# Two scalar loads moved to ScalarE's DMA queue, and the first rows loaded in four pieces

## What is computed

```python
x = x + jnp.tanh(g_xattn[0]) * _L0_xattn_ref(_layernorm(x), ctx_2048)
x = x + jnp.tanh(g_ffn[0]) * _L0_ffn_ref(_layernorm(x), Wg, w1, w2)
# _L0_xattn_ref: both operands rounded to fp8 by blocks, then a product
xq = quant_dequant_act_1x128(x)             # one scale for each row and 128 columns
wq = quant_dequant_weight_128x128(weight)   # one scale for each 128 by 128 block
return jnp.einsum('emk,enk->emn', xq, wq)
# _L0_ffn_ref: softmax router, top 2 of 8 experts, capacity 640 rows for each expert
h = jax.nn.relu(jnp.einsum('ecd,edf->ecf', dispatched, w1))
expert_out = jnp.einsum('ecf,efd->ecd', h, w2)
```

## Time and profile before

| | us |
|---|---|
| median of 3 runs (lowest, highest) | 882.12 (880.8, 883.58) |
| span of the profiled execution, first to last instruction | 888.7 |
| PE busy in the span | 812.6 (91%) |
| DVE busy | 606.8 (68%) |
| ACT busy | 365.3 (41%) |
| POOL busy | 236.2 (27%) |
| chain that ended last: PE, DVE, ACT, issue, DMA | 80%, 10%, 3%, 3%, 2% |

### The profile page before, as it was taken

How to read it: one execution, slowest core, us unless ns; L and a number is a source line. 1 busy time by engine, 2 the same in 40 slices (tenths; PEclk the granted TensorE clock), 3 DMA queues, 4 the chain that set the end, 5 groups by cost and what they waited for, 6 DMA issues and landing times.

```text
span 888.7 us, 12025 instructions
## 1 busy us (share of the span) xinstructions
PE 812.6 (91%) x4249; PEld 387.7 (44%) x4250; DVE 606.8 (68%) x988; ACT 365.3 (41%) x587; POOL 236.2 (27%) x210
## 2 busy tenths in 40 slices
PE   0277989689999999999999999999999999999996
PEld 0133558434444444444444444444444444444442
DVE  5999868847575778678677567757775777575430
ACT  3798996434142433344043314331433143314310
POOL 2133332565344014302320232023202320232010
PEclk9999996589999999999999999999999999999998
DMA  8600634485296329524843484347434743422000
GB/s 300 269 0 1 224 129 158 147 244 131 50 191 221 120 87 259 187 94 123 270 131 122 90 255 126 121 109 246 125 118 102 259 123 118 108 66 72 1 25 23
DMA packets 79033, 123.16 MB, mean 139 GB/s; under 512 B 43134, under 2 KB 43150, under 8 KB 74912
## 3 DMA queue, kind: packets, MB, share of 16 engines
q1 hardware_dynamic: 68032, 93.33, 34.1%
q0 software_dynamic: 10976, 29.50, 12.0%
HBM read 96.52 MB, written 18.95 MB: 130 GB/s over the span
## 4 chain that ended last, share of the span: by engine, by line
PE 80%; DVE 10%; ACT 3%; issue 3%; DMA 2%; POOL 1%; POOLq 0%; DVEq 0%; ACTq 0%
PE mm L840 38%; PE mm L770 36%; PE mm L810 2%; PE mm L550 2%; ACT region L895 1%; PE mm L749 1%; DVE region L1204 1%; DVE region L1215 1%; DMA gains<-in_g_ffn 1%; DVE region L1246 1%; DVE region L1242 1%; PE mm L578 1%; PE xT_ps L578 1%; PE mm L562 1%; DMA region<-x_split,row_next 1%
## 5 line engine op out<-in xcount | busy, mean ns | idle before, releaser
L840 PE MATMUL mm<-region,w_split 128*128 128x512 f16 x1536 | 337.3, 382 | 5.2 <-issue 3.7
L770 PE MATMUL mm<-region 128*128 128x512 f16 x1536 | 335.8, 379 | 0.0
L840 PEld LDWEIGHTS mm<-region,w_split 128*128 128x128 f16 x1536 | 151.0, 98 | 190.2 <-issue 12.0
L770 PEld LDWEIGHTS mm<-region 128*128 128x128 f16 x1536 | 148.9, 98 | 181.0 <-issue 3.8
L1123 ACT ACTIVATE region<-mm 128x512 f16<-128x512 f32 x128 | 76.4, 597 | 318.7 <-PE mm L840 309.7
L1545 DVE SCALAR_TENSOR_TENSOR region<-mm,region 128x512 f16<-128x512 f32 x128 | 88.5, 692 | 110.7 <-ACT region L1123 101.0
L476 POOL DMA_INDIRECT out<-region,back_now x40 | 63.9, 1598 | 172.5 <-DVE region L1558 141.9
L1548 DVE SCALAR_TENSOR_TENSOR region<-w_stage,w_scale,region 128x512 f16<-128x512 f32 x128 | 96.2, 752 | 0.0
L1126 ACT ACTIVATE region<-w_stage,w_scale 128x512 f16<-128x512 f32 x128 | 91.2, 712 | 0.0
L1333 DVE TENSOR_REDUCE top<-w_stage 128x1 f32<-128x512 f32 x112 | 76.0, 679 | 1.2 <-DMA w_stage<-in_L_ffn_w 1.2
L1342 DVE SCALAR_TENSOR_TENSOR w_split<-w_stage,w_scale,w_split 128x2048 f16<-128x2048 f32 x32 | 73.7, 2348 | 1.7 <-DVE region L1574 1.7
(11 more groups left out here) (197 smaller groups left out, 595.0 us busy)
## 6 DMA issues: line engine op xcount, KB each, us to landing
w_stage<-in_L_ffn_w SPq DMA_DIRECT2D x64, 1024.0 KB, 5.3
region<-in_x SPq DMA_DIRECT2D x4, 1024.0 KB, 13.8
x_split<-region SPq DMA_DIRECT2D x8, 512.0 KB, 3.1
out<-region SPq DMA_DIRECT2D x4, 1024.0 KB, 6.2
w_stage<-in_ctx SPq DMA_DIRECT2D x2, 1024.0 KB, 13.4
region<-in_ctx SPq DMA_DIRECT2D x2, 1024.0 KB, 15.7
region<-x_split,row_next POOLq DMA_INDIRECT x40
region<-out,row_next POOLq DMA_INDIRECT x40
```

What stands on the lines that cost most here:

```text
L770: mm = pe.matmul(mm2[s % 2][:, :], hidden[:, hh, f, s * P:(s + 1) * P], w2_split[:, wh, f, :], start=(f == 0 and hh + wh == 0), stop=(f == ...
L840: mm = pe.matmul(products(f), w1_split[:, wh, k, f * P:(f + 1) * P], xT[:, xh * KD + k, 0:WIDE], start=(k == 0 and wh + xh == 0), stop=(k ...
```

## The change

The two loads of the scalars leave POOL's list and stand at the head of ACT's, with a semaphore of their own, gains_in. ACT's tanh waits for those two loads and no longer for Wg; PE's router waits for Wg alone. The load of x of batch 0 becomes four loads of one tile (256 KB) each, with a semaphore each, and DVE waits for each tile just before its statistics. All other instructions and their order stay.

```diff
             for b in range(B):
-                sp.dma_start(x_all[:, b * MT:(b + 1) * MT, :], x_t[:, b * MT:(b + 1) * MT, :]).then_inc(x_in[b], 16)
+                if b == 0:
+                    for m in range(MT):
+                        sp.dma_start(x_all[:, m, :], x_t[:, m, :]).then_inc(x0_in[m], 16)
+                else:
+                    sp.dma_start(x_all[:, b * MT:(b + 1) * MT, :], x_t[:, b * MT:(b + 1) * MT, :]).then_inc(x_in[b], 16)
...
             pool.dma_start(wg_sb[:, :, :], wg_t).then_inc(q["consts_in"], 16)
-            pool.dma_start(gains[:, 0:1], g_xattn.unsqueeze(0).broadcast_to([P, 1])).then_inc(q["consts_in"], 16)
-            pool.dma_start(gains[:, 1:2], g_ffn.unsqueeze(0).broadcast_to([P, 1])).then_inc(q["consts_in"], 16)
...
                     if i == 0:
-                        pe.wait_ge(q["consts_in"], 48)
+                        pe.wait_ge(q["consts_in"], 16)
...
             def gain():
-                act.wait_ge(q["consts_in"], 48)
+                act.wait_ge(q["gains_in"], 32)
                 nc.scalar.activation(tanhs[:, :], gains[:, :], ACT.Tanh).then_inc(q["tanh_ready"], 1)
...
+            act.dma_start(gains[:, 0:1], g_xattn.unsqueeze(0).broadcast_to([P, 1])).then_inc(q["gains_in"], 16)
+            act.dma_start(gains[:, 1:2], g_ffn.unsqueeze(0).broadcast_to([P, 1])).then_inc(q["gains_in"], 16)
             gain()
             centre(0)
...
             def row_stats(b):
-                dve.wait_ge(x_in[b], 16)
+                if b > 0:
+                    dve.wait_ge(x_in[b], 16)
                 for m in range(MT):
+                    if b == 0:
+                        dve.wait_ge(x0_in[m], 16)
                     last = V.bn_stats(bn[:, m, :], x_tile(b, m))
```

More of the change, by code:

```diff
@@ L284, in build @@
         found_ps = marks_ps[:, 0:NS * 3].rearrange("p (s c) -> p s c", s=NS)
-        names = """consts_in w1_in0 w1_in1 w1_in2 w1_in3 w2_in0 w2_in1
+        names = """consts_in gains_in w1_in0 w1_in1 w1_in2 w1_in3 w2_in0 w2_in1
         w2_in2 w2_in3 rows_out split_out const_base consts tanh_ready prep
@@ L298, in build @@
         x_in = [sem(f"x_in{b}") for b in range(B)]
+        x0_in = [sem(f"x0_in{m}") for m in range(MT)]
         ctx_in_sem = [sem(f"ctx_in{b}") for b in range(B)]
```

## The result

The changed kernel takes 879.85 us (median of 8 runs, 879.21 to 880.35), the old one on the same chip 882.28 (880.56 to 883.58). The ratio is 0.9971, with a 95% interval of 0.9961 to 0.9981: 0.29% faster, 2.4 us by the medians and 2.6 by the ratio, clear of no change and almost exactly on the 0.3% that the prediction used as the line between "same" and "faster". The forecast was 879.3.

The account below looks back on a forecast made before the run. DVE bounds from the peaks of the context at 14.65 us, fed by the root and the context's landing. Root ready 11.7, context 11.8, so 882.12 - 2.85 = 879.3 us; range 876.7 less 0.2, to 882.6.

Parts of the forecast that it names:

- The bound and the way through: From the peaks of the context at 14.65 us DVE bounds without gap, so gains there reach ACT at 92.75.
- Rival (e): On PE at 144 to 148 us, a lower clock loses up to 1.4 us of the shift: 880.7 us; chance 0.11.
- The hole: DMA transfers slow from 7 to 11 us, 2.2 us missing on average, ascribed to 256 4-byte reads of the gains.
- rival (c): At the start, the transfer slowdown belonged to POOL's queue and is gone: 5.45 us earlier, 876.7 us; chance 0.22.
- The context at 11.8: Batch 0's context lands at 12.6 less 0.8, 11.8 us, starting its peaks 2.85 us earlier; chance 0.34.
- slow first microsecond: From 2 to 3 us only 70 GB/s move, so 0.8 us of the transfer slowdown falls on time already lost.
- so this costs nothing: SP's three more issues delay the context's issue to 2.9 us, free as DMA engines don't reach it before 6.5.
- The four statistics: On DVE, four tile loads hide 1.85 of 2.47 us of statistics; last tile to var_eps takes 1.31 us.
- (b): At the start, the transfer slowdown moves whole: context at 12.6, 2.05 us earlier, 880.1 us; chance 0.20.
- (d): At the start, each 4-byte piece is a packet of 0.40 us: context at 15.6, 0.95 us slower, 883.1; chance 0.13.
- The size: Whole kernel: 2.85 us off 882.12, forecast 879.3 us; chances faster 0.48, same 0.45, slower 0.07.

Follow-up runs that it names:

- the first form of the version with one read: Changed kernel with each scalar read once into one partition, tanh of two numbers, spread by PE, copied by DVE: 886.6 us, ratio 0.9960 to the old kernel.
- quiet start: Version with one read per scalar, POOL's Wg load and zeros store issued after its constants: ratio 0.9969, then 0.9972 (878.88 us); x in one load 0.9968 (879.3 us).

## Why the prediction was right, step by step

**The bound and the way through.** Right. L1215's start was the measure, the context was what fed it last (DVE waited 0.23 us for it), and 2.87 us at the start were 2.88 at the step to ACT, 2.92 at the first product of the expert part, and 2.4 to 2.6 in the times. Rival (e), a shift lost on the way to PE, did not show in this profiled execution, but it is real. In the second profiled execution of the changed kernel the step came at 89.50, 3.25 us before the old kernel's, and the first product of the expert part at 172.78, only 1.30 us before it. There PE's granted clock fell to 0.50, its lower level of 1.2 GHz, once more, where in the third it stayed at 1.00, with PE busy without a gap in both. The same stretch (columns of the earlier trace rows) in the second and in the third:

```profile
...
128.00:130.00 2.00, 2.00 (x4) 0.69 (x3) 1.52 (x8) 1.82 (x4) 0.00 (x0) 0.50 1.01 377
...
```

```profile
...
128.00:130.00 2.00, 2.00 (x6) 0.80 (x6) 1.50 (x9) 1.63 (x4) 0.00 (x0) 1.00 1.02 376
...
```

Of the 14 profiled executions three have this fall between 126 and 132 us, and the same three need 83.2 to 83.3 us from the step to the first product of the expert part, where the other eleven need 81.0 to 81.3. The other two are the first form of the version with one read and its quiet start with x in one load, so about 2 us of what those gained at the start was lost here in the trace. What decides whether the clock falls was not tried.

**The hole.** That the loads of the two gains made it was marked as a reading; it is shown now. Without the one address the hole is gone, with twice the reads it grows, and it lies in time behind the issue of those loads. It is one address read by all that does it, which I had only as an argument against rival (c).

**The context at 11.8.** It landed at 11.7, but two terms behind that number were off by about as much and cancelled, so that the sum came out so close was luck. First, I let 0.8 of the hole's 3.4 us fall on the slow first microsecond. In its new place the hole costs the context 1.9 us (9.0 without it, 10.9 with it, x in one load both times), against 3.6 before the change (12.6 less 9.0): 1.7 us were saved and not 0.8. (The 9.0 is from the quiet start, which also has Wg and the zeros out of the way; with four loads that moved the context from 10.65 to 10.35 and, in the second run, 9.95.) Why the same reads cost half as much there I can't say; the overlap with the start is one reading, the other queue is another. Secondly, "so this costs nothing", of the three more issues on SP, was wrong. In four loads the context lands 0.7 us later with the hole there (11.6 against 10.9) and 0.8 to 1.7 us later without it (9.8 to 10.7 against 9.0). That the DMA engines don't come to the context before 6.5 was a wrong reading too: up to 6.53 SP's queue had moved 1.37 MB in the old kernel, and x of batch 0 is 1.05 MB of it, so engines that were done with their share of x were already at the loads behind it. With the hole gone the transfers of 4 to 7 us run at 152 to 338 GB/s in four loads against 387 to 408 in one. What in the four loads does that is open.

**The four statistics.** That 1.85 us are hidden was right as a sum: from the last tile to var_eps it took 1.38 us (8.90 to 10.28), predicted 1.31. But the later landing of x (8.78 against 7.72) took 1.1 of it back, and with the context setting the start 0.54 us is what was left. Of the steps of the prediction this one held least; the total did not need it, because the context set the start.

**(b), the rule of the Trainium skill.** The prediction took from it (DMA: Bandwidth & Descriptors, the section "Issuing engines are not separate DMA queues") that DMAs of all issuers run on the same 16 engines. The trace agrees: the hole did not go, it moved from 7 to 11 us to 2 to 6 us. That it would then cost as much, which was my addition, did not hold.

**(c) and (d).** (c) is false as a cause: ACT's queue has the hole too. (d) had its mechanism half right, if each piece was a packet of its own, as the count has it. But the number of packets is not what makes the hole: in POOL's queue the same two loads are only 64 packets (10,976 in the page of the old kernel, 10,912 in that of the changed one), and the hole cost more there. The price that (d) put on a packet was far too high: with distinct addresses they left no hole from 2 to 5 us, and with one address 1.9 us over 16 is 0.12 us each, under the 0.34 at which it would have decided. The prediction also named what the Trainium skill (DMA: Bandwidth & Descriptors, "Specifications") states of transfers under 512 B, a read-modify-write. In the kernel with 256 places no price of that kind is to be seen; whether the engines did it no run here shows.

**The size.** Forecast 2.85 us, measured 2.4 to 2.6 in times and 2.87 in the trace. The result falls just short of the 2.65 us that the prediction took as the line between same (0.45) and faster (0.48).

## What to carry to other kernels

A scalar copied to 128 partitions by a broadcast read is no small load: here 256 reads of two addresses made the work behind them 1.5 to 3.6 us later, so issue it when nothing else is waited for, or read it once and spread it on the chip. The latter started the peaks 0.9 to 1.6 us sooner than the changed kernel, but no version with it was faster in time than the changed kernel by more than the noise. Splitting the first load hides the work on its first pieces, but it made the load behind it land later, and beside those reads the last piece too; weigh the two against each other. And an edit that moves one engine earlier can move it under another engine's work: look for short instructions that have become long. It can also meet another granted clock of PE: compare the same stretch of the traces before you believe a shift at the start.

## What was not expected of the hardware

- One address read 128 times by a DMA slows the transfers of the other queues: 37, 133 and 101 GB/s from 2 to 5 us, against 236, 279 and 313 on the same chip with 256 distinct addresses.
- By ACT's queue each 4-byte piece seems to be a packet of its own (288 packets for 256 pieces, 4 for two single reads); this alone left no hole.
- With the gains' reads beside it, x in four loads of 256 KB landed 1.1 us later than in one; the MB behind it landed 0.7 us later with those reads and 0.8 to 1.7 us later without (1.0 on one chip, 9.95 against 9.0).
- A 0.17 us instruction on DVE took 1.17 and 0.59 us while POOL made its identity matrices and counters, and ended within 0.03 us of POOL's last one.
- POOL's first identity matrix came at anything from 10.05 to 15.95 us, after a wait with no releaser in the profile; the same kernel, the quiet start with four loads, had it at 10.05 and at 13.96. It decides when such collisions happen.
- PE's granted clock fell to 0.50 between 126 and 132 us in three of 14 profiled executions, two of them of versions without the reads and one of the changed kernel, whose other two have no such fall; it cost about 2 us.
